# A feed forward phase whose slots close with the first layer's last product, and casts that follow their own gelu

## The chip, the cores and the metric

The kernel runs on one NeuronCore of one Trainium2 chip. The metric is the device time of one execution in microseconds. In this text PE is TensorE, DVE is VectorE, ACT is ScalarE, POOL is GpSimd and SP is SyncE, which here only issues DMA transfers.

## The reference

One transformer block over a batch of 32 sequences of 256 tokens, in fp32:

```
h = layernorm(x, ln1);  x = attention(h, h, sa_wq, sa_wk, sa_wv, sa_wo, sa_bo) + x
h = layernorm(x, ln2);  x = attention(h, ctx_768, ca_wq, ca_wk, ca_wv, ca_wo, ca_bo) + x
h = layernorm(x, ln3)
p = h @ ff_w1 + ff_b1                      # (256, 256) @ (256, 2048)
a, gate = p[..., :1024], p[..., 1024:]
x = (a * gelu(gate)) @ ff_w2 + ff_b2 + x   # (256, 1024) @ (1024, 256)
```

x is (32, 256, 256), the context (32, 256, 192), with 16 heads of 64. The change touches the last three lines only.

## The kernel before

A first phase, some 2300 us long, does both attentions for all batches and leaves x_ca in DRAM. A second phase does the feed forward, one batch (t) per iteration, 32 in all. Each engine's program is written by hand in its own order, and engines wait for each other by semaphores; nothing else sets the order of the work.

To keep fp32 accuracy, an operand is split into a high part, which PE can take in full (fp32r), and a remainder: hT_hi and hT_lo, w_hi and w_lo, a_hi and a_lo. One product of the mathematics is then three matmuls (high x high, high x low, low x high); `three` lists them. I call each matmul a product from here on. All of them here have a 128 x 128 stationary operand and 256 columns.

The 1024 hidden columns are cut into FT = 8 pieces. A slot of PE is one piece m: `hidden(t, m)` (12 products, into one of four banks of s_ps: 6 for the value half, 6 for the gate half), and `down`, which multiplies an earlier piece by its rows of ff_w2 (6 products: 3 into bank 0 of unit_ps for the first 128 tokens, 3 into bank 1 for the others, adding up over the 8 pieces). In slot m >= 2 it is down(t, m - 2), in slots 0 and 1 it is down(t - 1, 6) and down(t - 1, 7) of the batch before. The first iteration (START), which overlaps the end of attention, has an order of its own; the last (DRAIN) holds only the two last down pieces.

What hangs on a slot, with the semaphore that is raised:

- PE: the last product of hidden(m) raises p_full(m).
- ACT: `gelu(m)` waits for p_full(m), reads the gate half from s_ps and writes gate (gate_done). It is the line L895, ACT probs<-s_ps,b_col in the profile, since gate and hid lie in the buffer probs.
- DVE: `gated(m)` (L1080) adds the bias to the value half and multiplies by the gate into hid (hid_done).
- ACT: `hidden_hi(m)` (L900), the cast of hid to a_hi (u_hi). In the order of ACT it stands behind gelu(m + 1).
- POOL: `hidden_lo(m)` (L1268), a_lo = hid - a_hi (u_lo).
- PE: down(m), two slots on, waits for u_lo(m).

Other work of an iteration stands at fixed places of these orders. DVE: behind gated(0) it normalises the rows of batch t + 1 and transposes blocks of them (L1005, L1012); behind gated(1) it adds the residual to both banks of the finished batch t - 1 into x_out (L1202, y_done); behind gated(4) scale_rows (L1087, hT); behind gated(5) the statistics of batch t + 2 (L992); ahead of gated(6) the remainder hT_lo (L1094, rows_lo); behind gated(6) the moments mean_var (L997). ACT: behind the cast that follows gelu(5), the cast of hT to hT_hi (L904, `rows_hi`). POOL: behind a_lo(3) the residual addition x_rb (L1240, waits for the load of x_res); ahead of a_lo(6) `deviation` of batch t + 2 (var_eps, neg_mean, rstd, ln_shift, L1229 to L1234), in iterations 1 to 29. SP stores x_out when y_done allows, and loads x_res when that store has landed.

down(t, 0) starts a new sum in the banks of unit_ps, so it also waits for y_done: both additions of batch t - 1 must have read them. hidden(m) waits for hid_done(m - 4), the last reader of its bank.

## Time and profile before

| | us |
|---|---|
| median of 3 runs | 2865.33 (2865.15 to 2866.21) |
| the profiled execution | 2866.01 |
| its span, first to last instruction | 2864.2 |
| PE busy in the span | 2842.0, 25278 matmuls |
| DVE, ACT, POOL busy | 2256.3, 1912.3, 1471.1 |
| the feed forward stretch 2340 to 2844, PE busy | 504.00 of 504.00 |

The profile is of one execution. Start times are measured; the ends of matmuls are modelled, so the distance from one start to the next tells how fast products follow each other, and not the duration that stands with them (0.28 us). An engine's time without work is "idle"; a row shows in brackets how long the engine was idle ahead of it and who ended that.

### The profile page before, as it was taken

Reading aid. Unit: us, or ns where it says so; the run is one execution under the profiler, and the core shown is the slowest. Engines: PE = TensorE matmul, PEld = TensorE weight load, DVE = VectorE, ACT = ScalarE, POOL = GpSimd, SP = SyncE. Lnnn points to the kernel's source line nnn. Section 1 sums busy time; section 2 is a strip of 40 time slices with the busy share of each in tenths; the row PEclk is TensorE's granted clock in tenths of the full one; section 3 lists DMA queues with packets and bytes.
Section 4 is the critical chain, followed back from the end, with each engine's and each line's share of the span. In section 5 each row is a group of like instructions: output and inputs, shape, how many; then the busy total and the mean of one; then the engine's idle time right before and its main releaser. Section 6 shows DMA issues by size and latency. Waiting matters only on the chain.

```text
span 2864.2 us, 72446 instructions
## 1 busy us (share of the span) xinstructions
PE 2842.0 (99%) x25278; PEld 2485.3 (87%) x25278; DVE 2256.3 (79%) x3495; ACT 1912.3 (67%) x6041; POOL 1471.1 (51%) x1310
## 2 busy tenths in 40 slices
PE   8999999999999999999999999999999999999999
PEld 6888888888888888888888888888888889999999
DVE  6888888888888888888888888888888865555554
ACT  6677766677766776777777777777777754444443
POOL 5444444444444444765555555555555544554554
PEclk9999999999999999999999999999999999999999
DMA  5666666666666666667777776666766632222222
GB/s 147 158 162 157 156 157 159 158 154 145 151 151 154 150 148 149 161 166 177 177 172 169 173 171 169 168 164 165 168 168 163 151 100 88 73 73 84 81 73 63
DMA packets 355360, 413.32 MB, mean 144 GB/s; under 512 B 122048, under 2 KB 209472, under 8 KB 355264
## 3 DMA queue, kind: packets, MB, share of 16 engines
q1 hardware_dynamic: 345120, 395.29, 57.4%
q10 hardware_dynamic: 10144, 16.78, 1.6%
q8 instruction: 56, 0.92, 0.1%
q14 instruction: 40, 0.33, 0.0%
HBM read 94.52 MB, written 49.02 MB: 50 GB/s over the span
## 4 chain that ended last, share of the span: by engine, by line
PE 98%; DVE 1%; ACT 1%; POOL 0%; issue 0%; DMA 0%; DVEq 0%; POOLq 0%; ACTq 0%
PE unit_ps L593 54%; PE o_ps L618 17%; PE s_ps L606 14%; PE s_ps L593 12%; DVE neg_max L1021 0%; ACT probs L851 0%; DVE blocks L1035 0%; POOL probs L1253 0%; DMA x_ln<-in_x_dram 0%; ACT qk_hi L882 0%; DVE qk_lo L1046 0%; DVE hT L1016 0%; DVE hT_lo L1059 0%; ACT x_n L828 0%; ACT L828 0%
## 5 line engine op out<-in xcount | busy, mean ns | idle before, releaser
L1253 POOL TENSOR_TENSOR probs<-probs,row_inv 128x1024 f32<-128x1024 f32 x512 | 967.8, 1896 | 893.9 <-DVE row_inv L1026 893.9
L851 ACT ACTIVATE probs<-s_ps,neg_max 128x256 f32<-128x256 f32 x2048 | 950.4, 487 | 403.9 <-DVE neg_max L1021 403.4
L1021 DVE TENSOR_REDUCE neg_max<-s_ps 128x4 f32<-128x1024 f32 x512 | 616.8, 1205 | 62.8 <-PE s_ps L606 58.4
L1035 DVE STREAM_TRANSPOSE blocks<-probs 128x1024 f32<-128x1024 f32 x512 | 633.2, 1237 | 19.9 <-POOL probs L1253 19.9
L593 PE MATMUL unit_ps<-hT_hi,w_hi 128*128 128x256 f32 x2048 | 571.3, 282 | 3.0 <-DVE hT_lo L1059 2.6
L593 PE MATMUL unit_ps<-hT_hi,w_lo 128*128 128x256 f32 x2048 | 554.0, 277 | 0.0
L618 PE MATMUL o_ps<-pT,v_f 128*64 128x256 f32 x4096 | 498.5, 385 | 1.7 <-DVE a_lo L1041 1.7
L593 PE MATMUL unit_ps<-hT_lo,w_hi 128*128 128x256 f32 x1792 | 496.1, 277 | 0.0
L851 ACT ACTIVATION_READ_ACCUMULATOR probs<-s_ps,neg_max 128x1 f32 x2048 | 444.6, 217 | 0.0
L593 PE MATMUL unit_ps<-w_hi,a_hi 128*128 128x256 f32 x1536 | 430.8, 280 | 3.8 <-DVE a_lo L1041 2.8
L593 PE MATMUL unit_ps<-w_lo,a_hi 128*128 128x256 f32 x1536 | 425.7, 277 | 0.0
L593 PE MATMUL unit_ps<-w_hi,a_lo 128*128 128x256 f32 x1536 | 425.7, 277 | 0.0
L618 PEld LDWEIGHTS o_ps<-pT,v_f 128*64 128x64 f32 x4096 | 271.7, 136 | 174.6 <-issue 48.0
L1046 DVE TENSOR_TENSOR qk_lo<-unit_ps,qk_hi 128x512 fp32r<-128x512 f32 x512 | 350.8, 685 | 76.8 <-ACT qk_hi L882 62.5
L593 PEld LDWEIGHTS unit_ps<-hT_hi,w_hi 128*128 128x128 f32 x2048 | 384.3, 188 | 21.2 <-issue 1.5
L593 PEld LDWEIGHTS unit_ps<-hT_hi,w_lo 128*128 128x128 f32 x2048 | 384.6, 188 | 0.0
L593 PEld LDWEIGHTS unit_ps<-hT_lo,w_hi 128*128 128x128 f32 x1792 | 336.8, 188 | 5.7
L1268 POOL TENSOR_TENSOR a_lo<-probs,a_hi 128x256 fp32r<-128x256 f32 x256 | 188.3, 741 | 264.9 <-ACT a_hi L900 263.0
L895 ACT ACTIVATE probs<-s_ps,b_col 128x256 f32<-128x256 f32 x256 | 121.7, 476 | 300.2 <-PE s_ps L593 300.2
L606 PE MATMUL s_ps<-qk_hi 64*128 64x256 f32 x2048 | 315.2, 304 | 6.0 <-DVE qk_lo L1046 6.0
L882 ACT CAST qk_hi<-unit_ps 128x512 fp32r<-128x512 f32 x512 | 313.9, 613 | 6.4 <-PE unit_ps L593 4.6
L1080 DVE SCALAR_TENSOR_TENSOR probs<-s_ps,b_col,probs 128x256 f32<-128x256 f32 x256 | 123.4, 482 | 240.7 <-ACT probs L895 238.7
(73 smaller groups left out, 6017.8 us busy)
## 6 DMA issues: line engine op xcount, KB each, us to landing
pT<-blocks SPq DMA_DIRECT2D x1024, 256.0 KB, 4.5
rows_t_dram<-row_blocks SPq DMA_DIRECT2D x91, 256.0 KB, 4.4
rows_in<-rows_t_dram SPq DMA_DIRECT2D x91, 256.0 KB, 4.1
x_res<-in_x_dram SPq DMA_DIRECT2D x32, 256.0 KB, 4.1
x_sa_dram<-x_out SPq DMA_DIRECT2D x32, 256.0 KB, 4.3
x_ln<-x_sa_dram ACTq DMA_DIRECT2D x32, 256.0 KB, 4.9
ctx_in<-in_ctx_dram SPq DMA_DIRECT2D x32, 256.0 KB, 4.4
x_res<-x_sa_dram SPq DMA_DIRECT2D x32, 256.0 KB, 4.1
```

Of the source, the lines that this page charges most:

```text
L593: last = nc.tensor.matmul(dst, a, b, start=start and n == 0, stop=stop and n == len(terms) - 1)
L606: last = nc.tensor.matmul(s_ps[:, m % 2, hd, it * S:(it + 1) * S], q[part, r, 0, rows], k[part, r, 1, :], start=n == 0, stop=n == 2)
L618: last = nc.tensor.matmul(o_ps[part, i, :], v_f[:, jt, 2 * (2 * n + i) + hd, :], p[:, jt, hd], start=jt == 0, stop=jt == IT - 1)
L851: op = nc.scalar.activation(probs[:, m % 2, r, :].rearrange("p (j b c) -> p j b c", j=IT, c=BLK), scored.rearrange("p (j c b) -> p j b c", ...
L882: nc.scalar.copy(qk_hi[:, unit[1] % RING, :, :], bank.rearrange("p (a s) -> p a s", a=2)).then_inc(at.qk_hi, 1)
L895: nc.scalar.activation(gate[:, m % 2, :], s_ps[:, m % 4 // 2, m % 2, S:2 * S], ACT.Gelu, bias=b1_col[:, FT + m:FT + m + 1]).then_inc(ff.ga ...
L1021: nc.vector.tensor_reduce(neg_max[:, m % RING, :], s_ps[:, m % 2, :, :].rearrange("p h (i j) -> p (h i) j", j=S), AX_X, ALU.max, negate=Tr ...
L1035: nc.vector.transpose(blocks[:, n % 2, :, m % 2, :].rearrange("p b (j r c) -> p r j b c", j=IT, c=BLK), probs[:, m % 2, :, :].rearrange("p ...
L1046: nc.vector.tensor_tensor(qk_lo[:, m % RING, :, :], unit_ps[:, bank_of(("qk", m)), :].rearrange("p (a s) -> p a s", a=2), f32(qk_hi[:, m % ...
L1080: nc.vector.scalar_tensor_tensor(hid[:, m % 2, :], s_ps[:, m % 4 // 2, m % 2, 0:S], b1_col[:, m:m + 1], gate[:, m % 2, :], ALU.add, ALU.mu ...
L1253: nc.gpsimd.tensor_tensor(probs[:, m % 2, :, :], probs[:, m % 2, :, :], row_inv[:, m % RING, :].unsqueeze(2).broadcast_to([P, ROWS, S]), A ...
L1268: nc.gpsimd.tensor_tensor(a_lo[:, m, :], hid[:, m % 2, :], f32(a_hi[:, m, :]), ALU.subtract).then_inc(ff.u_lo, 1)
```

## The change

Three things change, all in the iterations of the feed forward behind the first:

- PE: hidden and down of a slot are no longer one behind the other. A slot is now 11 products of hidden, 5 of down, the last product of hidden (which raises p_full), the last product of down. The waits of down (u_lo, and for down(t, 0) also y_done) stand ahead of its first product, now the 12th of the slot. The number of products and their sums' order within each bank stay as they are.
- ACT: hidden_hi(m) now follows gelu(m), and not gelu(m + 1). At m = 5 the rows' cast rows_hi stands between the two.
- The first (START) and the DRAIN iteration keep their order, of PE and, in START, of ACT.

```
-            def hidden(t, m, parity):
...
+            def hidden_and_down(t, m, parity, b, d):
+
+                hidden_ready(t, m)
+                wide, narrow = hidden_terms(t, m, parity), down_terms(d)
+                run_terms(wide[:-1])
+                down_ready(b, d)
+                last = run_terms(narrow[:3])
+                if d == FT - 1:
+                    last.then_inc(ff.w2_full, 1)
+                run_terms(narrow[3:-1])
+                run_terms(wide[-1:]).then_inc(ff.p_full, 1)
+                last = run_terms(narrow[-1:])
+                if d == FT - 1:
+                    last.then_inc(ff.w2_full, 1)
...
                 for m in range(FT):
-                    if "cur" in parts and not (parts == START and m < BEGUN):
+                    if parts != START and "cur" in parts:
+                        hidden_and_down(t, m, parity, t if m >= 2 else t - 1, (m - 2) % FT)
+                        continue
+                    if "cur" in parts and m >= BEGUN:
                         hidden(t, m, parity)
...
                         gelu(t, m)
-                        if m:
+                        if parts == START:
                             hidden_hi(t, m - 1)
-                        if m == FT - 1:
-                            hidden_hi(t, m)
                     if "nxt" in parts and m == (FT - 2 if parts == START else FT - 3):
                         rows_hi(t + 1, 1 - parity)
+                    if "cur" in parts and (parts != START or m == FT - 1):
+                        hidden_hi(t, m)
```

`hidden_ready` and `down_ready` hold the waits that stood at the top of `hidden` and `down`, `hidden_terms` and `down_terms` list their 12 and 6 products in the order of before, and `run_terms` issues a list.

PE, in an iteration, from the last products of hidden(1) over down(t - 1, 7) to the start of slot 2; unit_ps<-w,a is down, s_ps<-hT,w is hidden. Before:

```order
L593 MATMUL s_ps<-hT_lo,w_hi 128x256
L593 MATMUL s_ps<-hT_hi,w_lo 128x256
L593 MATMUL unit_ps<-w_hi,a_hi 128x256 [waits ff_u_lo]
L593 MATMUL unit_ps<-w_lo,a_hi 128x256
L593 MATMUL unit_ps<-w_hi,a_lo 128x256
L593 MATMUL unit_ps<-w_hi,a_hi 128x256
L593 MATMUL unit_ps<-w_lo,a_hi 128x256
L593 MATMUL unit_ps<-w_hi,a_lo 128x256
L593 MATMUL s_ps<-hT_hi,w_hi 128x256 [waits ff_hid_done]
```

The same place in the changed kernel:

```order
L709 MATMUL s_ps<-hT_lo,w_hi 128x256
L709 MATMUL unit_ps<-w_hi,a_hi 128x256 [waits ff_u_lo]
L709 MATMUL unit_ps<-w_lo,a_hi 128x256
L709 MATMUL unit_ps<-w_hi,a_lo 128x256
L709 MATMUL unit_ps<-w_hi,a_hi 128x256
L709 MATMUL unit_ps<-w_lo,a_hi 128x256
L709 MATMUL s_ps<-hT_hi,w_lo 128x256
L709 MATMUL unit_ps<-w_hi,a_lo 128x256
L709 MATMUL s_ps<-hT_hi,w_hi 128x256 [waits ff_hid_done]
```

The product s_ps<-hT_hi,w_lo that raises p_full has moved down by five, and all of down but its last product has moved up by one. In slot 2 the first product of down also waits for ff_y_done, in both kernels.

ACT, from gelu(4) to gelu(6) of an iteration (ACTIVATE is gelu, CAST a_hi is hidden_hi, CAST hT_hi is rows_hi). Before:

```order
L895 ACTIVATE probs<-s_ps,b1_col 128x256 [waits ff_hid_done,ff_p_full]
L900 CAST a_hi<-probs 128x256 [waits ff_hid_done]
L895 ACTIVATE probs<-s_ps,b1_col 128x256 [waits ff_hid_done,ff_p_full]
L900 CAST a_hi<-probs 128x256 [waits ff_hid_done]
L904 CAST hT_hi<-hT 128x512 [waits ff_h_done]
L895 ACTIVATE probs<-s_ps,b1_col 128x256 [waits ff_hid_done,ff_p_full]
```

The same stretch in the changed kernel:

```order
L936 ACTIVATE probs<-s_ps,b1_col 128x256 [waits ff_hid_done,ff_p_full]
L941 CAST a_hi<-probs 128x256 [waits ff_hid_done]
L936 ACTIVATE probs<-s_ps,b1_col 128x256 [waits ff_hid_done,ff_p_full]
L945 CAST hT_hi<-hT 128x512 [waits ff_h_done]
L941 CAST a_hi<-probs 128x256 [waits ff_hid_done]
L936 ACTIVATE probs<-s_ps,b1_col 128x256 [waits ff_hid_done,ff_p_full]
```

The cast behind each gelu is now that of the same m, where it was that of m - 1; the one that belongs to gelu(5) stands behind the rows' cast.

## Rows read from the trace of the kernel before

**Rows 1.** The page: PE's busy time, its clock in 40 slices, the chain by engine.
```profile
PE 2842.0 (99%) x25278; PEld 2485.3 (87%) x25278; DVE 2256.3 (79%) x3495; ACT 1912.3 (67%) x6041; POOL 1471.1 (51%) x1310
...
PEclk9999999999999999999999999999999999999999
...
PE 98%; DVE 1%; ACT 1%; POOL 0%; issue 0%; DMA 0%; DVEq 0%; POOLq 0%; ACTq 0%
```

**Rows 2.** Busy us (x instructions) by engine, clock, DMA share, GB/s, 2340 to 2844.
```profile
2340.00:2844.00 504.00, 504.00 (x4343) 504.00 (x4342) 277.60 (x597) 207.49 (x512) 252.72 (x392) 1.00 0.26 78
```

**Rows 3.** PE's timeline, slots 1 and 2: start us, duration, engine, line, operation.
```profile
2526.01 0.28 PE L593 MATMUL s_ps<-hT_hi,w_hi 128*128 128x256 f32 x1
...
2527.31 0.28 PE L593 MATMUL s_ps<-hT_hi,w_lo 128*128 128x256 f32 x1
...
2528.14 0.28 PE L593 MATMUL s_ps<-hT_hi,w_hi 128*128 128x256 f32 x1
...
2529.39 0.28 PE L593 MATMUL s_ps<-hT_hi,w_lo 128*128 128x256 f32 x1
```

**Rows 4.** DVE's timeline: gated(1), x_out twice; scale_rows behind gated(4); mean_var behind gated(6).
```profile
2528.14 0.48 DVE L1080 SCALAR_TENSOR_TENSOR probs<-s_ps,b_col,probs 128x256 f32<-128x256 f32 x1
2528.54 0.74 DVE L1202 TENSOR_TENSOR x_out<-unit_ps,x_rb 128x256 f32<-128x256 f32 x2
...
2534.80 2.13 DVE L1087 TENSOR_SCALAR hT<-rows_in,ln_gain,ln_bias 128x256 f32<-128x256 f32 x2
...
2539.02 0.24 DVE L997 BATCH_NORM_AGGREGATE mean_var<-bn 128x2 f32<-128x6 f32 x2
```

**Rows 5.** PE's timeline: the start of slot 3, and down(6) in the next slot 0.
```profile
2530.19 0.28 PE L593 MATMUL s_ps<-hT_hi,w_hi 128*128 128x256 f32 x1
...
2542.05 0.28 PE L593 MATMUL unit_ps<-w_hi,a_hi 128*128 128x256 f32 x1
```

**Rows 6.** POOL's timeline: a_lo(0), the residual, the deviation's start, a_lo(6), the program's last.
```profile
2528.47 0.74 POOL L1268 TENSOR_TENSOR a_lo<-probs,a_hi 128x256 fp32r<-128x256 f32 x1 [2.74 <-ACT a_hi L900]
...
2535.43 1.35 POOL L1240 TENSOR_TENSOR x_rb<-x_res,out_bias 128x512 f32<-128x512 f32 x1
...
2539.61 0.20 POOL L1229 TENSOR_TENSOR var_eps<-mean_var,eps 128x2 f32<-128x2 f32 x1
...
2541.01 1.44 POOL L1268 TENSOR_TENSOR a_lo<-probs,a_hi 128x256 fp32r<-128x256 f32 x2
...
2858.67 1.42 POOL L1268 TENSOR_TENSOR a_lo<-probs,a_hi 128x256 fp32r<-128x256 f32 x2 [1.34 <-ACT a_hi L900]
```

**Rows 7.** ACT's timeline: gelu(1), the cast behind it, the rows' cast, the last cast.
```profile
2527.63 0.48 ACT L895 ACTIVATE probs<-s_ps,b_col 128x256 f32<-128x256 f32 x1 [1.54 <-PE s_ps L593]
2528.00 0.40 ACT L900 CAST a_hi<-probs 128x256 fp32r<-128x256 f32 x1
...
2536.96 0.62 ACT L904 CAST hT_hi<-hT 128x512 fp32r<-128x512 f32 x1 [0.21 <-DVE hT L1087]
...
2858.85 0.40 ACT L900 CAST a_hi<-probs 128x256 fp32r<-128x256 f32 x1 [0.26 <-DVE probs L1080]
```

**Rows 8.** PE's timeline at the program's end: down products behind a wait.
```profile
2859.45 0.39 PE L593 MATMUL unit_ps<-w_hi,a_hi 128*128 128x256 f32 x1 [0.98 <-POOL a_lo L1268]
2859.68 0.28 PE L593 MATMUL unit_ps<-w_lo,a_hi 128*128 128x256 f32 x1
2859.80 0.28 PE L593 MATMUL unit_ps<-w_hi,a_lo 128*128 128x256 f32 x1
```

**Rows 9.** SP's timeline: the load of x_res is issued.
```profile
2531.68 0.38 SPq L578 DMA_DIRECT2D x_res<-x_ca_dram  x1
```

**Rows 10.** PE's timeline where the phases meet: the products behind a long wait.
```profile
2313.05 0.55 PE L593 MATMUL unit_ps<-w_hi,a_hi 128*128 128x256 f32 x1 [2.81 <-DVE a_lo L1041]
2313.40 0.41 PE L593 MATMUL unit_ps<-w_lo,a_hi 128*128 128x256 f32 x1
...
2315.32 0.41 PE L593 MATMUL unit_ps<-w_lo,a_hi 128*128 128x256 f32 x1
```

More of the change, by code:

```diff
@@ L702, in down, with hidden @@
                     at_least(pe, ff.y_done, IT * b)
-                for it, bank in enumerate((unit_ps[:, 0, :], unit_ps[:, 1, :])):
-                    rows = slice(it * P, (it + 1) * P)
-                    last = product(bank[:, 0:D], three(a_hi[:, m, rows], a_lo[:, m, rows],
-                                                       w_hi[:, 2, m * D:(m + 1) * D], w_lo[:, 2, m * D:(m + 1) * D]),
-                                   start=m == 0, stop=m == FT - 1)
+            def hidden(t, m, parity):
+                hidden_ready(t, m)
+                run_terms(hidden_terms(t, m, parity)).then_inc(ff.p_full, 1)
+            def down(b, m):
+                down_ready(b, m)
+                terms = down_terms(m)
+                for part in (terms[:3], terms[3:]):
+                    last = run_terms(part)
                     if m == FT - 1:
                         last.then_inc(ff.w2_full, 1)
+            def hidden_and_down(t, m, parity, b, d):
+                hidden_ready(t, m)
+                wide, narrow = hidden_terms(t, m, parity), down_terms(d)
[9 more added lines that the diff above has]
+                    last.then_inc(ff.w2_full, 1)
             def transpose_rows(b):
@@ L776, in iteration @@
                         pe.wait_ge(ff_w2_lo, 1)
-                    if "cur" in parts:
-                        for d in {4: (0,), 5: (1,), 6: (2, 3), 7: (4, 5)}.get(m, ()) if parts == START else (m - 2,) if m >= 2 else ():
+                    if parts == START:
+                        for d in {4: (0,), 5: (1,), 6: (2, 3), 7: (4, 5)}.get(m, ()):
                             down(t, d)
@@ L967, in iteration @@
                         gelu(t, m)
-                        if m:
+                        if parts == START:
                             hidden_hi(t, m - 1)
-                        if m == FT - 1:
-                            hidden_hi(t, m)
                     if "nxt" in parts and m == (FT - 2 if parts == START else FT - 3):
                         rows_hi(t + 1, 1 - parity)
+                    if "cur" in parts and (parts != START or m == FT - 1):
+                        hidden_hi(t, m)
             over_batches(act, B, iteration)
```

32 lines of the change are left out of this document (23 added, 9 removed).

## The prediction

> **What bounds the kernel now.** I read the page's engine table and its chain of waits first: TensorE (PE) is busy 99% of the span and is 98% of the chain that ended last [rows 1]. Then the busy time of the feed forward stretch, which is all that the change touches: from 2340 to 2844 us PE is busy in all 504.00 us, with 4343 products at a granted clock of 1.00, while VectorE (DVE) has 278, ScalarE (ACT) 207 and GpSimd (POOL) 253 us [rows 2]. So nothing waits on PE's side, and a product costs 504.0 / 4343 = 0.116 us. An iteration is 8 slots x 18 products = 144 products, or 16.7 us. That leaves two ways for the order of products to cost or gain: it changes how fast products follow each other, or it makes PE wait for data that today arrive just in time. I call the product that raises p_full(m) "p(m)": before, it is the 12th of slot m, after, the 17th.
>
> The reader is to see in PE's own rows how little is spare. In the slot m = 2 shown, the last product ahead of down(0) starts at 2529.39, and with it the load of down(0)'s weights [rows 3]. down(0) overwrites the two banks that DVE's x_out additions read, so it waits for y_done, and the second addition ends at 2528.54 + 0.74 = 2529.28 [rows 4]. The spare time is 0.11 us. Slot m = 0 is alike: down(6) begins at 2542.05 [rows 5], its load a product earlier, at 2541.93, and the remainder a_lo of product 6, the first of a pair that takes 1.44 us in sum from 2541.01 [rows 6], ends near 2541.75: 0.18 us spare.
>
> **Part 1: p_full comes 5 products later.** No product is added or taken away. p(m) moves from place 12 to place 17, so it comes 5 x 0.116 = 0.58 us later in its slot, and gelu(m), gated(m) and everything behind them on DVE shift with it. At the same time down's first product moves from place 13 to place 12, so its data are needed 0.12 us earlier. Together: everything that hangs on p(m) and is needed by a down product loses 0.70 us. What hung on p(m-1) and is now cut loose from it is part 2.
>
> The addition that frees the banks is hit in full. Its chain: p(1) starts at 2527.31 [rows 3], gelu(1) at 2527.63 [rows 7], gated(1) at 2528.14, the two additions to 2529.28 [rows 4]; that is 1.97 us from p(1). DVE's order puts the additions of iteration t behind gated(t, 1) and the change leaves this so; the casts on ACT play no part. Before, p(1) to the load of down(0) is 18 products, 2529.39 - 2527.31 = 2.08 us. After, it is from place 17 of slot 1 to the start of the 11th product of slot 2, 12 products, 12 x 0.116 = 1.39 us. PE is late by 1.97 - 1.39 = 0.58 us. A product that waited starts 0.04 us after its release: the a_lo pair that ends at 2858.67 + 0.74 = 2859.41 for its first [rows 6] lets PE go at 2859.45, and the next product follows 0.23 us on [rows 8]; in the stream it is also two products, 0.23 us, from the start of a load to that next product, so nothing more is lost. Stall: 0.58 + 0.05 (with rounding) = 0.63 us. It stands in every iteration that has both a current and a previous batch, 31 of 32: **31 x 0.63 = 19.5 us**. Behind the waiting product are queued 4 more of down(0) and p(2); so gelu(2) comes later too, but slots 2 to 7 keep their distances, and nothing is caught up, since PE has no idle time in which to do so.
>
> **Part 2: each cast follows its own gelu.** Before, cast(m-1) is run after gelu(m). Left so, a_lo(m) would end 2.0 us after p(m+1) (from p(1) at 2527.31 to 2528.47 + 0.74 = 2529.21 is 1.90 [rows 3, 6]) against 1.39 us given, and all slots would stall by 0.5 us. With cast(m) behind gelu(m), the chain for a clean m is, from p(m): 0.32 to gelu, 0.51 to gated, 0.48 for gated, 0.03 and 0.40 for the cast (as after the last gated, [rows 7]), 0.07 to POOL (2528.00 + 0.40 to 2528.47), 0.74 for a_lo: 2.55 us [rows 3, 4, 6, 7]. It is given from place 17 of slot m to place 11 of slot m+2, 30 products, 3.48 us. So 0.9 us is spare, and the cast costs nothing in a clean slot: ACT is idle there for 1.54 us of a slot [rows 7]. Three slots are not clean:
>
> m = 4: the residual addition on POOL stands ahead of a_lo(4). Its input x_res is asked for at 2531.68 [rows 9], 4.37 us after p(1), and has landed by 2535.43 [rows 6], 8.12 us after p(1). Now p(1) to p(4) is 3 slots and the stall, 6.9 us, so the addition starts at the latest 1.2 us after p(4), takes 1.35, and a_lo(4) ends at 3.3 us after p(4), where 3.48 are given. No cost.
>
> m = 5: ACT now runs the rows' cast, which waits for scale_rows (hT), ahead of cast(5). p(4) is 73 products ahead of the product at 2542.05 [rows 5], at 2533.58; hT ends at 2534.80 + 2.13 = 2536.93 [rows 4], 3.35 us after it; the rows' cast adds 0.65, cast(5) 0.40, a_lo(5) 0.81 [rows 6, 7]: 5.2 us from p(4), 3.1 from p(5), against 3.48. No cost, 0.4 us spare.
>
> m = 6: POOL's deviation of batch t+2 (var_eps to ln_shift) stands ahead of a_lo(6), and it waits for DVE's mean_var, which stands behind gated(6). p(6) lies 37 products ahead of the one at 2542.05 [rows 5], at 2537.75. From there mean_var ends at 2539.02 + 0.24 = 2539.26, or 1.51 [rows 4]; POOL picks it up 0.07 later, at 1.58 (before, it was busy with a_lo(5) until 2539.61; that cover is gone since a_lo(5) now comes earlier); from var_eps to a_lo is 2541.01 - 2539.61 = 1.40, giving 2.98; a_lo(6) takes 0.74: 3.72; with 0.05 for the release 3.77 us [rows 6]. Given are 3.48. Stall: 0.29 us, in the iterations t = 1 to 29, which are those with a deviation: **29 x 0.29 = 8.4 us**. Its bounds: 0.2 if POOL picks up at once and rows_lo no longer holds gated(6) back by 0.05 us, 0.4 if each semaphore takes 0.05 more.
>
> **Part 3: the end.** The last batch's gelu(7) comes 0.58 us later; its a_lo(7), queued until 2860.09 behind a_lo(6) today [rows 6], ends at 2858.85 + 0.58 (the cast's new start [rows 7]) + 0.48 + 0.74 = 2860.65: **0.6 us** at the end.
>
> **Part 4: the pace.** Slots alternate: the one from 2526.01 takes 2.13 us and the next, from 2528.14, 2.05 us (products 0.118 and 0.113 apart) [rows 3, 5]. The turn comes at a slot's first product, where PE goes from unit_ps to s_ps, whichever pace it leaves; at the opposite crossing none is seen. The new order has two crossings of each kind per slot. I can't derive what it does: if each crossing to s_ps turns the pace, 16 of 18 products keep the pace of the slot before, and all may be fast or all slow. After a wait, a down product restarts at 0.118 [rows 8], which speaks for slow. Of 144 products, 42 (12 and 30) lie in the two stretches whose length the chains set, so the pace counts in 102: all fast gives 31 x 8 x 0.037 x 102 / 144 = -6.5 us, all slow +6.5 us, alternating 0. I take 0, since both ends have the same reach, and keep both for the range.
>
> **The sum.** 19.5 + 8.4 + 0.6 + 0 = 28.5 us on the profiled execution's own time of 2866.01 us (span 2864.2 and 1.8 around it), 2894.5 us. The median of the runs, 2865.33, lies 0.7 below that execution: **2893.8 us**, or 1.0% slower.
>
> **The rivals.**
> (a) Both stalls, all slots slow: 2893.8 + 6.5 = 2900 us. For it: the restart pace, and two turns in a slot, which would keep a pace once taken. Against: that slots alternate today.
> (b) Both stalls, all slots fast: 2887 us.
> (c) Only the y_done stall, because mean_var reaches POOL sooner: 2893.8 - 8.4 = 2885 us. Against it: the 1.40 us from var_eps to a_lo are POOL's own.
> (d) At the start of the phase 9 products take 2315.32 - 2313.40 = 1.92 us, 0.2133 us each [rows 10], at half speed. The pace falls to half of that, 0.1067 us: the new order would take out what makes them 0.113 or 0.118 at full speed. 102 x 31 x 0.0094 = 29.7 us are given back, and the kernel ends at 2864 us, **not slower**; the deciding pace is 0.116 - 28.5 / 3162 = 0.107 us. Against it: no row of the stretch shows such a pace for 256 columns with a load for each. The Trainium skill ("TensorE: Matmul & The Clock Gate", on the back-to-back issue gap) gives N / 2.4 GHz + 2.5 ns and says that loading the next weights steals nothing from the running matmul, which would be 0.109 us whatever the order; the trace shows 0.113 and 0.118 here, so the rule does not hold for this stream. With that figure the estimate would be 2872 us.
> (e) More stalls than I found, or the clock: after an idle time of 2.81 us PE's products come 0.213 us apart, at half their pace [rows 10]. A stall of 0.63 us is far from that, and the page shows 9 tenths or more in each slice of the clock's row [rows 1], but if each stall brought some of it, 2905 to 2960 us.
> (f) The change doing nothing: excluded, the order of PE and ACT differs in each slot.
>
> **How the numbers follow.** Forecast with mixed pace 0.55 (2889 to 2899); (a) 0.13; (b) 0.12; (c) 0.08; (d) 0.05, half of it near 2872, half near 2864; (e) 0.06; 0.01 for some faster way. The range leaves out (d), (e) and a little of (a): 2884 to 2904. A measurement of this kernel tells 0.2% (5.7 us, 2859.6 to 2871.1) from no change; slower 0.94, same 0.04, faster 0.02.
>
> **What would show it.** In the changed profile, PE should have idle time put down to DVE x_out in slot 2 (31 times, near 0.6 us) and to POOL a_lo in slot 0 (29 times, near 0.3); PE busy in the same stretch should fall to about 95%; iterations should last 17.6 us, not 16.7; var_eps should start about 0.07 after mean_var. The gelu should start in the slot's last product. Wrong would be: no PE wait on x_out, which breaks the largest term; waits in other slots, which means that a chain was missed; slots that all last 2.05 or 2.13 us, which decides part 4.

## The result, and the profile after

| | before | after |
|---|---|---|
| median, us | 2865.33 (2864.28 to 2866.85, 5 executions) | 2895.32 (2893.77 to 2895.58, 5 executions) |
| the profiled execution | 2866.01 | 2895.32 |
| its span | 2864.2 | 2893.5 |

The changed kernel takes 1.0103 times as long, interval 1.0089 to 1.0117. The forecast was 2893.8 us in a range of 2884 to 2904.

The page of the changed kernel: PE's line of the engine table, its clock in 40 slices, the chain by engine and by line. They answer [rows 1].

```profile
PE 2862.0 (99%) x25278; PEld 2493.0 (86%) x25278; DVE 2251.0 (78%) x3495; ACT 1931.2 (67%) x6041; POOL 1468.7 (51%) x1310
...
PEclk9999999999999999999999999999999999999999
...
PE 96%; DVE 2%; ACT 1%; issue 1%; POOL 0%; DMA 0%; DVEq 0%; POOLq 0%; ACTq 0%
PE unit_ps L593 48%; PE o_ps L618 16%; PE s_ps L606 14%; PE s_ps L709 11%; PE unit_ps L709 7%; DVE x_out L1243 1%; ACT probs L936 1%; DVE neg_max L1062 0%; ACT probs L892 0%; DVE blocks L1076 0%; POOL probs L1294 0%; DMA x_ln<-in_x_dram 0%;
```

The clock's row has not changed, the number of products neither. What is new is in the chain: PE had 98% of it and has 96%, and DVE's x_out, which was not in it, has 1%.

PE's waits in the feed forward phase of the changed kernel: in total, times, the longest.

```profile
PE unit_ps L709 <- DVE x_out L1243: 10.7, 31, 0.5
PE unit_ps L709 <- POOL a_lo L1309: 1.1, 1, 1.1
```

The 31 waits for x_out are there. The 29 waits for a_lo in slot 0 are not (the one listed is that of the program's end), and the 31 are listed at 0.35 us each in the mean and not at 0.6. Both come from the same thing: the end of a product is modelled at 0.28 us behind its start, while in the stream the next one starts after 0.116. A wait shows as idle time only by what it exceeds this 0.16 us. The list of the weight loads (PEld), from 2340 to 2880, has both:

```profile
PEld unit_ps L709 <- DVE x_out L1243: 15.1, 28, 0.6
PEld unit_ps L709 <- POOL a_lo L1309: 6.0, 29, 0.2
PEld unit_ps L709 <- issue: 1.8, 3, 0.6
```

28 and 3 (which the profile puts down to no releaser) are the 31 of slot 2, and the 29 of slot 0 are there. A load shows as taking 0.19 us, so these times are too short as well; for the size of a stall the starts have to be read. PE's timeline of the changed kernel around slot 2 of one iteration: start us, duration, engine, line, operation, idle before. It answers [rows 3].

```profile
2520.82 0.28 PE L709 MATMUL s_ps<-hT_hi,w_lo 128*128 128x256 f32 x1
...
2521.05 0.28 PE L709 MATMUL s_ps<-hT_hi,w_hi 128*128 128x256 f32 x1
...
2522.23 0.28 PE L709 MATMUL s_ps<-hT_lo,w_hi 128*128 128x256 f32 x1
2522.85 0.39 PE L709 MATMUL unit_ps<-w_hi,a_hi 128*128 128x256 f32 x1 [0.33 <-DVE x_out L1243]
2523.07 0.28 PE L709 MATMUL unit_ps<-w_lo,a_hi 128*128 128x256 f32 x1
...
2531.92 0.28 PE L709 MATMUL s_ps<-hT_hi,w_lo 128*128 128x256 f32 x1
...
2535.41 0.28 PE L709 MATMUL s_ps<-hT_lo,w_hi 128*128 128x256 f32 x1
2535.69 0.39 PE L709 MATMUL unit_ps<-w_hi,a_hi 128*128 128x256 f32 x1
2535.92 0.28 PE L709 MATMUL unit_ps<-w_lo,a_hi 128*128 128x256 f32 x1
```

2520.82 is p(1). From the last product ahead of down(0) to down(0) is 2522.85 - 2522.23 = 0.62 us and to the next product 0.22 more, 0.84 in all where the stream takes 0.23: the stall is 0.61 us. p(6) is at 2531.92, and down(6) at 2535.69 comes 0.28 us after its predecessor and 0.23 ahead of its successor, 0.51 in place of 0.23: a stall of 0.28 us with no bracket behind it.

From here on a stall is this: the time from the last product ahead of down's first to the second of down, less 0.23 us.

The chain of the first stall, DVE and then ACT, same kernel and view; it answers [rows 4, 7].

```profile
2521.65 0.48 DVE L1121 SCALAR_TENSOR_TENSOR probs<-s_ps,b_col,probs 128x256 f32<-128x256 f32 x1
2522.05 0.74 DVE L1243 TENSOR_TENSOR x_out<-unit_ps,x_rb 128x256 f32<-128x256 f32 x2
...
2521.14 0.47 ACT L936 ACTIVATE probs<-s_ps,b_col 128x256 f32<-128x256 f32 x1 [0.47 <-PE s_ps L709]
2522.16 0.41 ACT L941 CAST a_hi<-probs 128x256 fp32r<-128x256 f32 x1 [0.55 <-DVE probs L1121]
```

gelu(1) starts 0.32 us after p(1), gated(1) 0.51 later, the additions end at 2522.05 + 0.74 = 2522.79, 1.97 us after p(1), to the hundredth what it was before. PE starts 0.06 us later. The cast at 2522.16 isn't in this chain.

The chain of the second: POOL, then DVE, same kernel. It answers [rows 4, 6]; a_lo(5) is the row at 2531.63, a_lo(6) the one at 2534.89.

```profile
2528.13 1.29 POOL L1281 TENSOR_TENSOR x_rb<-x_res,out_bias 128x512 f32<-128x512 f32 x1
...
2531.63 0.73 POOL L1309 TENSOR_TENSOR a_lo<-probs,a_hi 128x256 fp32r<-128x256 f32 x1 [1.34 <-ACT a_hi L941]
2533.54 0.20 POOL L1270 TENSOR_TENSOR var_eps<-mean_var,eps 128x2 f32<-128x2 f32 x1 [1.18 <-DVE mean_var L1038]
...
2534.89 0.75 POOL L1309 TENSOR_TENSOR a_lo<-probs,a_hi 128x256 fp32r<-128x256 f32 x1
...
2528.96 1.49 DVE L1128 TENSOR_SCALAR hT<-rows_in,ln_gain,ln_bias 128x256 f32<-128x256 f32 x2
...
2531.81 1.11 DVE L1135 TENSOR_TENSOR hT_lo<-hT,hT_hi 128x512 fp32r<-128x512 f32 x1
2532.84 0.47 DVE L1121 SCALAR_TENSOR_TENSOR probs<-s_ps,b_col,probs 128x256 f32<-128x256 f32 x1
2533.24 0.23 DVE L1038 BATCH_NORM_AGGREGATE mean_var<-bn 128x2 f32<-128x6 f32 x2
```

POOL had been idle for 1.18 us when mean_var released it, 0.07 us after its end; a_lo(6) ends at 2535.64, 3.72 us after p(6).

At the end, on POOL and then PE, same kernel: the last remainder and the product that waits for it ([rows 6, 8] before).

```profile
2888.72 0.72 POOL L1309 TENSOR_TENSOR a_lo<-probs,a_hi 128x256 fp32r<-128x256 f32 x1 [1.38 <-ACT a_hi L941]
...
2889.49 0.38 PE L709 MATMUL unit_ps<-w_hi,a_hi 128*128 128x256 f32 x1 [1.13 <-POOL a_lo L1309]
```

The whole difference of the two profiled executions, 29.3 us, can be laid out from the starts:

| where | us |
|---|---|
| slot 2, 31 stalls, 27 of them 0.61 and four 0.63 to 0.69 | 19.1 |
| slot 0, 29 stalls of 0.27 to 0.30 | 8.1 |
| the pace of the products: from the second slot of the phase to the last slot 7 are 554.75 us and not 526.40, less the stalls | 1.1 |
| from the start of the last slot 7 to the last product, 5.17 and not 4.60 | 0.6 |
| ahead of the changed code (the second slot of the phase starts at 2330.25 and not 2329.85) | 0.4 |
| sum | 29.3 |

### The profile page after: what moved, and what is told of

Its sections match the earlier page's. It is cut to its first block, busy times and chain, and to the rows that moved or that the text cites. A ratio compares the mean times of both kernels' runs of the same rounds, so it can differ in the third digit from the quotient of the medians.

```text
span 2893.5 us, 72446 instructions
## 1 busy us (share of the span) xinstructions
PE 2862.0 (99%) x25278; PEld 2493.0 (86%) x25278; DVE 2251.0 (78%) x3495; ACT 1931.2 (67%) x6041; POOL 1468.7 (51%) x1310
## 4 chain that ended last, share of the span: by engine, by line
PE 96%; DVE 2%; ACT 1%; issue 1%; POOL 0%; DMA 0%; DVEq 0%; POOLq 0%; ACTq 0%
PE unit_ps L593 48%; PE o_ps L618 16%; PE s_ps L606 14%; PE s_ps L709 11%; PE unit_ps L709 7%; DVE x_out L1243 1%; ACT probs L936 1%; DVE neg_max L1062 0%; ACT probs L892 0%; DVE blocks L1076 0%; POOL probs L1294 0%; DMA x_ln<-in_x_dram 0%; ACT qk_hi L923 0%; PE unit_ps L796 0%; DVE probs L1121 0%
## 5 line engine op out<-in xcount | busy, mean ns | idle before, releaser
L902 ACT CAST a_hi<-o_ps 128x512 fp32r<-128x512 f32 x256 | 153.6, 600 | 210.9 <-PE o_ps L618 210.1
L593 PE MATMUL unit_ps<-w_hi,a_hi 128*128 128x256 f32 x1024 | 287.8, 281 | 2.8 <-DVE a_lo L1082 2.8
L606 PE MATMUL s_ps<-qk_lo,qk_hi 64*128 64x256 f32 x2048 | 289.0, 279 | 0.0
L606 PE MATMUL s_ps<-qk_hi,qk_lo 64*128 64x256 f32 x2048 | 288.2, 278 | 0.0
```

Source lines behind the costliest of these rows:

```text
L593: last = nc.tensor.matmul(dst, a, b, start=start and n == 0, stop=stop and n == len(terms) - 1)
L606: last = nc.tensor.matmul(s_ps[:, m % 2, hd, it * S:(it + 1) * S], q[part, r, 0, rows], k[part, r, 1, :], start=n == 0, stop=n == 2)
L902: nc.scalar.copy(a_hi[:, 2 * n:2 * n + 2, :], o_ps[:]).then_inc(at.a_hi_done, 1)
```

## The experiments

All times in us, the kernel before beside each on the same chip (its medians lay between 2865.15 and 2865.76). The ratio is to it, with its interval; it is an estimate from all executions and need not be the quotient of the two medians.

| kernel | median (lowest to highest, executions) | ratio |
|---|---|---|
| e3_casts_alone | 2866.75 (2865.50 to 2867.16, 10) | 1.0004 (0.9994 to 1.0013) |
| e4_products_alone | 2988.12 (2987.68 to 2988.56, 2) | 1.0425 (1.0404 to 1.0446) |
| e1_additions_first | 2885.57 (2883.64 to 2888.27, 4) | 1.0068 (1.0051 to 1.0085) |
| e2_remainder_first | 2870.17 (2868.13 to 2871.37, 10) | 1.0015 (1.0006 to 1.0025) |
| e8_rows_remainder_later | 2886.53 (2883.67 to 2886.83, 4) | 1.0070 (1.0053 to 1.0087) |
| e5_two_of_down | 2880.95 (2875.98 to 2882.08, 4) | 1.0056 (1.0039 to 1.0073) |
| e5b_two_of_down_again | 2877.49 (2876.17 to 2879.65, 3) | 1.0043 (1.0027 to 1.0059) |
| e6_before_one_wait_less | 2866.37 (2863.91 to 2866.55, 10) | 1.0002 (0.9992 to 1.0012) |
| e7_both_mended_one_wait_less | 2869.68 (2869.11 to 2872.72, 10) | 1.0018 (1.0009 to 1.0028) |
| e9_mended_three_of_down | 2867.50 (2866.93 to 2868.59, 10) | 1.0006 (0.9997 to 1.0016) |
| e10_mended_four_of_down | 2875.38 (2872.93 to 2878.83, 6) | 1.0035 (1.0022 to 1.0048) |
| e11_mended_two_of_down | 2864.41 (2862.67 to 2874.24, 12) | 1.0009 (0.9999 to 1.0018) |

### The two halves of the change apart

The casts alone, on the kernel before:

```
-                        if m:
+                        if parts == START:
                             hidden_hi(t, m - 1)
-                        if m == FT - 1:
-                            hidden_hi(t, m)
...
+                    if "cur" in parts and (parts != START or m == FT - 1):
+                        hidden_hi(t, m)
```

> The kernel before, with only ACT's part of the change: each cast follows its own gelu, PE's order is that of before. Theory: casts cost nothing and gain nothing, since PE did not wait for a_lo: 2865.3 us (2864 to 2867), within 0.1% of before. The end is the same too, since the last a_lo hangs on gelu(7). Rival (ACT waiting for gated delays gelu or the rows' cast, and so PE): 2 to 10 us slower.

Measured: 2866.75 us, within the range given, and no difference that can be told. One thing did move: hT_lo on DVE takes 1.24 us (median of 30) where it took 0.69, since a_lo(5) now runs beside it on POOL. That it costs nothing shows how much room the old order of products leaves on that side.

The products alone, the changed kernel with ACT's old order:

```
-                        if parts == START:
+                        if m:
                             hidden_hi(t, m - 1)
+                        if m == FT - 1:
+                            hidden_hi(t, m)
...
-                    if "cur" in parts and (parts != START or m == FT - 1):
-                        hidden_hi(t, m)
```

> The changed kernel with ACT's order of before: cast(m-1) behind gelu(m), only the products are moved. Theory: a_lo(m-1) ends 1.90 us after p(m), with 0.05 for the release 1.95, and 12 products = 1.39 us are given, so every slot of 31 iterations stalls by 0.56 us, slot 2 by 0.63, slot 0 a little more for the deviation: 31 x (7 x 0.56 + 0.63) + 2 = 143 us over before, about 3008 us (2995 to 3025). Rival (the cast's place is of no weight, the cost is in the products' order and y_done): within 5 us of 2895.

PE's waits in this kernel over the whole span:

```profile
PE unit_ps L709 <- POOL a_lo L1309: 54.6, 186, 1.5
PE unit_ps L709 <- DVE x_out L1243: 10.9, 31, 0.4
```

Measured: 2988.12 us, 20 less than expected. The size of a stall was right, 0.55 us from start to start. Their number was not: 186 is 6 x 31, and with slot 2 that makes 7 of 8 slots. Slot 1, which takes down(t - 1, 7), runs through, because in the old order too the cast of the last piece stands right behind its own gelu(7). 31 x (6 x 0.555 + 0.61) = 122 us; measured are 123.0 over the kernel before. So the order of casts is worth nothing by itself and 93 us under the new order of products (2988.1 to 2895.3): the change needs both halves, and the loss is that of the products.

### The slot-2 stall, and what stood behind it

The two additions ahead of gated(t, 1) on DVE, in the changed kernel:

```
+                    if m == 1 and "prv" in parts:
+                        dve.wait_ge(ff.xrb_done, t)
+                        for it, bank in enumerate((unit_ps[:, 0, :], unit_ps[:, 1, :])):
+                            dve.wait_ge(ff.w2_full, IT * (t - 1) + it + 1)
+                            nc.vector.tensor_tensor(x_out[:, it, :], bank[:, 0:D], x_rb[:, it, :], ALU.add).then_inc(ff.y_done, 1)
                     if "cur" in parts and not (parts == START and m < BEGUN):
                         gated(t, m)
...
-                    if m == 1 and "prv" in parts:
...
```

> The changed kernel, but on DVE the two x_out additions of batch t-1 stand ahead of gated(t, 1), not behind it. Theory (two chains hung on p_full make PE wait): the y_done wait of slot 2 goes. The second addition now waits only for the last product of slot 1 and ends about 0.28 + 0.04 + 0.42 = 0.74 us after its start, where 11 products = 1.28 us are given. The changed kernel's profile has 31 gaps of 0.61 us over a normal step there, 18.8 us: 2895.3 - 18.8 = 2876.5 us (2875 to 2878). Rival (the mixed order of products is itself slow, and the waits only fall where PE is late anyway): the time stays within 3 us of 2895.

PE's waits in e1 from 2330 to 2890:

```profile
PE unit_ps L709 <- POOL a_lo L1309: 10.0, 24, 1.1
```

The timeline of e1 in one iteration, POOL's rows and then DVE's. x_rb is the residual addition of the iteration's own batch, hT is scale_rows:

```profile
2507.41 1.29 POOL L1281 TENSOR_TENSOR x_rb<-x_res,out_bias 128x512 f32<-128x512 f32 x1 [0.69 <-DMA x_res<-x_ca_dram]
...
2510.63 0.73 POOL L1309 TENSOR_TENSOR a_lo<-probs,a_hi 128x256 fp32r<-128x256 f32 x1 [1.19 <-ACT a_hi L941]
2512.54 0.20 POOL L1270 TENSOR_TENSOR var_eps<-mean_var,eps 128x2 f32<-128x2 f32 x1 [1.18 <-DVE mean_var L1038]
...
2507.50 2.10 DVE L1128 TENSOR_SCALAR hT<-rows_in,ln_gain,ln_bias 128x256 f32<-128x256 f32 x2
...
2510.68 1.23 DVE L1135 TENSOR_TENSOR hT_lo<-hT,hT_hi 128x512 fp32r<-128x512 f32 x1
2511.84 0.47 DVE L1121 SCALAR_TENSOR_TENSOR probs<-s_ps,b_col,probs 128x256 f32<-128x256 f32 x1
```

Measured: 2885.57 us, 9 more than expected. The wait for x_out is gone, as expected, and 10 us are gone with it, not 19. The stall in slot 0 has grown: by the starts it is between 0.17 and 0.88 us, 16.5 us over 29 iterations or 0.57 in the mean, where it was 0.28; in this iteration down(6) comes 0.72 us after its predecessor (2513.95 to 2514.67). The rows show why. p(6) is at 2510.47 here. gated(6) starts 1.37 us after it, and 0.92 us after it in the changed kernel. Of these 0.45 us, 0.32 are a later start of hT_lo (0.21 after p(6), not 0.11 ahead of it) and 0.12 its longer run (1.23, not 1.11). The later start goes back to scale_rows: here POOL's residual addition waits for the load of x_res, and seen from p(4), two slots ahead of p(6), it starts 0.7 us later than in the changed kernel, where the stall of slot 2 had given the load time. It now lies beside the whole of scale_rows (2507.41 beside 2507.50, hT in 2.10 us), where in the changed kernel it began 0.83 us ahead of it (2528.13 and 2528.96, hT in 1.49 us). In slot 2 0.05 to 0.08 us are left over in 28 iterations (2.1 us in all), since the additions there stand behind the transposes of slot 0.

The 0.32 and 0.12 are read off one iteration; the cause shows in all 29 of this trace. In 22 of them x_rb starts 0.86 to 1.30 us after p(4), and the later it starts the longer is the stall of slot 0, nearly one for one: 0.47 us at 0.86, 0.61 at 1.01, 0.78 at 1.19, 0.88 at 1.30. In one it starts 0.40 us after p(4), as in the changed kernel, and the stall is 0.28. In the other six the load lands so late that x_rb starts 1.31 us or more after p(4) and scale_rows has begun ahead of it, at 1.23 us; hT then takes 1.73 us or less and the stall is 0.26 us or less. One of these six, POOL's row and then DVE's:

```profile
2490.59 1.28 POOL L1281 TENSOR_TENSOR x_rb<-x_res,out_bias 128x512 f32<-128x512 f32 x1 [1.02 <-DMA x_res<-x_ca_dram]
2490.30 1.73 DVE L1128 TENSOR_SCALAR hT<-rows_in,ln_gain,ln_bias 128x256 f32<-128x256 f32 x2
```

So the stall of slot 0 in e1 is set by when the load of x_res lands, which the stall of slot 2 had hidden. Whether hT_lo is the part that decides was tried next but one.

e2: the same, and on POOL the remainder ahead of the deviation:

```
+                    if "cur" in parts:
+                        hidden_lo(t, m)
                     if m == FT - 2 and rows_ahead(t, parts) and parts != START:
                         deviation(ff, t + 2)
-                    if "cur" in parts:
-                        hidden_lo(t, m)
```

> As the first, and on POOL a_lo(6) stands ahead of the deviation of batch t+2, not behind it. Theory: the slot 0 stall, 29 gaps of 0.28 us, 8.1 us, goes too: 2868.4 us (2866.5 to 2870), which leaves about 0.6 us for the end and 1 to 2 us for the extra crossings between the two sets of banks. No PE wait is left in the stretch. Rival (the order of products costs by itself): 2876 or more.

Measured: 2870.17 us. This is just above the range given. With both stalls out of the way, the new order of products costs 5.0 us. In the profiled execution 4.8 us lie between the two kernels: 2.0 are the 0.07 us left in slot 2 28 times, 0.7 five waits in slot 6, 1.3 the pace, 0.5 the end, and 0.3 lie ahead of the changed code. So the two chains named in the prediction are nearly all there was: from the changed kernel to this one are 25 us, and the two terms had 27.9.

The waits in slot 6 are a third chain, that of the prediction's m = 4: the load of x_res, x_rb, a_lo(4), down(4). The longest of them, on POOL and then on the weight loads:

```profile
2352.28 1.45 POOL L1281 TENSOR_TENSOR x_rb<-x_res,out_bias 128x512 f32<-128x512 f32 x1 [1.21 <-DMA x_res<-x_ca_dram]
2354.49 0.19 PEld L709 LDWEIGHTS unit_ps<-w_hi,a_hi 128*128 128x128 f32 x1 [0.30 <-POOL a_lo L1309]
```

Here x_rb starts 1.65 us after p(4), and the stall is 0.37 us; the four others are 0.09 us. In the changed kernel, where the stall of slot 2 comes first, x_rb starts at most 0.59 us after p(4) and slot 6 never waits.

e8: e1, and DVE's hT_lo behind gated(6) and the moments:

```
-                    if (m == FT - 2 and by_blocks(t, parts)) or (m == FT - 1 and parts == START):
+                    if m == FT - 1 and parts == START:
                         rows_lo(t + 1, 1 - parity)
...
                     if m == FT - 2 and rows_ahead(t, parts):
                         norm_moments(ff)
+                    if m == FT - 2 and by_blocks(t, parts):
+                        rows_lo(t + 1, 1 - parity)
```

> The kernel with the x_out additions ahead of gated(1) (e1_additions_first, 2885.6 us, 9 us above what its theory gave, with a new PE wait of 0.5 to 0.7 us on a_lo(6) in slot 0), and on DVE rows_lo of batch t+1 now behind gated(6) and the moments, not ahead of them. Theory C (rows_lo, drawn out to 1.20 us where POOL's a_lo(5) runs beside it, against 0.69 us alone, holds gated(6) back, and through the deviation a_lo(6)): gated(6) starts 0.83 us after p_full(6)'s product and not 1.37, the wait in slot 0 shrinks from about 0.6 to about 0.25 us, and 29 x 0.3 to 0.5 us are given back: 2874 us (2871 to 2878). Rival (the wait comes from POOL's own order, which the deviation fills): 2884 to 2887.

The timeline of e8 where mean_var meets the deviation, DVE's rows and then POOL's:

```profile
2513.06 0.24 DVE L1038 BATCH_NORM_AGGREGATE mean_var<-bn 128x2 f32<-128x6 f32 x2
2513.22 0.66 DVE L1135 TENSOR_TENSOR hT_lo<-hT,hT_hi 128x512 fp32r<-128x512 f32 x1
...
2513.38 0.55 POOL L1272 TENSOR_TENSOR var_eps<-mean_var,eps 128x2 f32<-128x2 f32 x1 [0.53 <-DVE mean_var L1038]
```

The deviation's first operation over all iterations of e8 (min, median, max in ns):

```profile
L1272 POOL TENSOR_TENSOR var_eps<-mean_var,eps x29: 548/550/552, 2356.8 to 2843.8; 128x2 f32<-128x2 f32 x29
```

Measured: 2886.53 us, the rival's number. hT_lo no longer holds gated(6), and takes 0.66 us and not 1.24. But the operation of two columns that follows on POOL, 0.20 us in every other kernel here, takes 0.55, for it starts inside hT_lo and ends 0.05 us behind its end (2513.88 and 2513.93). The stall in slot 0 is 0.55 us, 16.0 us over all, where e1 had 16.5; it is now nearly alike in all iterations (0.52 to 0.60 us), whenever the load lands. The cost was moved from one engine to the other. So hT_lo on DVE and var_eps on POOL can't run side by side, and in the two places tried for hT_lo something ahead of a_lo(6) is late; what removed the stall was to take the deviation from ahead of a_lo(6) (e2).

### p_full a little earlier

e5: the last product of hidden after 2 products of down and not 5. The edit, in hidden_and_down of the changed kernel:

```
-                last = run_terms(narrow[:3])
+                run_terms(narrow[:2])
+                run_terms(wide[-1:]).then_inc(ff.p_full, 1)
+                last = run_terms(narrow[2:3])
...
-                run_terms(narrow[3:-1])
-                run_terms(wide[-1:]).then_inc(ff.p_full, 1)
-                last = run_terms(narrow[-1:])
+                last = run_terms(narrow[3:])
```

> The changed kernel with the last product of hidden moved three places up: 11 of hidden, 2 of down, the last of hidden (place 14), the last 4 of down. Theory (lateness grows product by product): from p_full(1) to down(0)'s load are now 15 products = 1.74 us against the chain of 2.02, a stall of 0.27 us in slot 2, 31 x 0.27 = 8.4 us; in slot 0 33 products = 3.83 us against 3.77, no stall. 2865.3 + 8.4 + 0.4 for the end + 1 for the crossings = 2875 us (2873 to 2878). If DVE's rows_lo is again drawn out by POOL's a_lo beside it, slot 0 adds up to 29 x 0.3 us, 2884. Rival (the order of products costs by itself, wherever p_full stands): 2890 or more.

> e5_two_of_down once more, for a second profile: its runs lay between 2876 and 2882 us, and its profile, of a 2876 run, showed 141 slots of 2.08 us and 56 of 2.12. Theory: the pace that a slot settles in differs between executions, the difference of 5 us being some 130 more slots of 2.12 us. If this profile is of a run near 2881, it has 100 or more slots of 2.12 us, or else more waiting; if it is near 2876 it looks as the first.

Measured: 2880.95 and, once more, 2877.49 us. Three products (0.35 us) given back per slot take the slot-2 stall from 0.61 to 0.28 us in the mean (0.25 to 0.35, 8.6 us in all), and the time falls by 14 to 18 us. In slot 0 the stall is gone in about half of the iterations; 16 have one of 0.04 to 0.58 us, 2.9 us in all (13 and 2.2 us in the second profile), and as in e1 it is there when x_rb starts late. The direction and the stall are as the chains say. The time lies between what the two readings gave, and its spread over seven executions, 6 us, is wider than any other's up to here. The second profile, of the 2877.49 us execution, has 84 slots of 2.12 and 2.13 us where the first, of 2875.98 us, has 60, some 1.0 us of the 1.5 between them; no execution above 2880 us was profiled, so the spread was not settled here. The next kernels bear on it.

### The pace

Two ideas of what turns the pace at a slot's first product were set against each other with e6: the wait for hid_done that stands there, or the order of products itself. e6 is the kernel before and e7 is e2, each with that wait in the first iteration only (the order of the bank is kept without it: down of the slot before has waited for an a_lo that comes after that hid_done). The edit of e6; in e7 the same line reads `t * FT + m - 3`:

```
-                at_least(pe, ff.hid_done, g - 3)
+                if t == 0 if isinstance(t, int) else False:
+                    at_least(pe, ff.hid_done, g - 3)
```

> The kernel before, without PE's wait for hid_done at each slot's first product, behind the first iteration (it is implied: down of the slot before has waited for the a_lo that follows that hid_done). No other edit. Theory A (the wait on the first load of a slot is what turns the pace between 0.113 and 0.118 us): all slots keep one pace, 2865.3 - 9.2 = 2856 us if all are fast, 2874.5 if all are slow. Theory B (going from unit_ps to s_ps, that is from down to hidden, turns it): the slots alternate as before, 2865 us within 1.5 us.

> The kernel with both stalls mended (x_out additions ahead of gated(1), a_lo(6) ahead of the deviation, measured 2870.2 us), and without the hid_done wait. Theory A: one pace throughout, about 2861 or 2879 us. Theory B: 2870 us within 1.5 us.

Measured: 2866.37 and 2869.68 us, each the same as the kernel it was made from, and the slots of e6 still last 2.05 and 2.13 us in turn (122 of each). The wait doesn't turn the pace.

e9, e10 and e11 are e2 with the last product of hidden after 3, 4 and 2 products of down:

```
-                run_terms(narrow[3:-1])
                 run_terms(wide[-1:]).then_inc(ff.p_full, 1)
-                last = run_terms(narrow[-1:])
+                last = run_terms(narrow[3:])
```

(e9; in e10 `narrow[3:4]` stays ahead of it, e11 has e5's edit.)

> Both mends (additions ahead of gated(1), a_lo(6) ahead of the deviation), and the slot is 11 of hidden, 3 of down, the last of hidden, 3 of down. Theory D (a crossing from down to hidden turns the pace if enough products follow; three turn it back before the next slot's first product): no waits, slots of 2.076 us each instead of 2.053 and 2.127 in turn, 248 x (2.090 - 2.076) = 3.5 us less and 0.35 us more at the end: 2862 us, or 2872 if slots settle in the slow pace (2.116 us). Rival (the turn is tied to the slot and not to the crossing): slots alternate, 2867 us.

> As e9_mended_three_of_down with 4 of down ahead of the last of hidden and 2 behind it. Theory D with two products enough for a turn: slots of 2.072 us, 2861 us. If two are too few: slots of 2.067 and 2.126 us in turn, as in the changed kernel, 2867 us.

> Both mends (additions ahead of gated(1), a_lo(6) ahead of the deviation), and the slot is 11 of hidden, 2 of down, the last of hidden, 4 of down. No waits are expected. What the pace does was not foretold right for 3 and 4 of down (slots of 2.07 and 2.12 us in turn; all of 2.13). With 2 of down the profiles of e5 show slots that keep 2.08 us until a wait throws them into 2.12. Theory D: without waits all keep 2.08: 2865.5 - 248 x 0.010 + 0.25 = 2863 us. If they settle at 2.12: 2873 us. Rival (without the waits they alternate like the others): 2867 us.

Busy us (x instructions) by engine from 2500 to 2840, of e2, e9, e10 and e11, in this order, one fence each; PE's count is the number of products that fit into 340 us.

```profile
2500.00:2840.00 340.00, 340.00 (x2910) 339.87 (x2910) 192.14 (x401) 152.68 (x344) 168.97 (x263) 1.00 0.26 79
```

```profile
2500.00:2840.00 340.00, 340.00 (x2922) 340.00 (x2921) 193.50 (x406) 153.90 (x346) 170.31 (x263) 1.00 0.26 78
```

```profile
2500.00:2840.00 340.00, 340.00 (x2872) 340.00 (x2871) 191.06 (x400) 150.96 (x339) 166.50 (x259) 1.00 0.26 76
```

```profile
2500.00:2840.00 340.00, 340.00 (x2945) 340.00 (x2944) 193.97 (x406) 154.76 (x348) 172.01 (x265) 1.00 0.26 78
```

The same stretch of the kernel before, and of the changed one:

```profile
2500.00:2840.00 340.00, 340.00 (x2931) 340.00 (x2929) 189.45 (x406) 140.78 (x347) 170.64 (x264) 1.00 0.26 78
```

```profile
2500.00:2840.00 340.00, 333.61 (x2776) 325.51 (x2774) 176.27 (x388) 145.76 (x328) 160.43 (x250) 1.00 0.25 73
```

With no wait in this stretch, e9, e10 and e11 still differ. The lengths of slots, from start to start, with how many there are from 2340 us to the last slot (246 or 247):

| kernel | slots |
|---|---|
| before | 2.05 (123), 2.08 (1), 2.13 (123) |
| changed | 2.06 to 2.08 (121), 2.12 and 2.13 (66); with a stall 2.39 and 2.40 (29), 2.72 to 2.77 (31) |
| e9 (3 of down ahead) | 2.07 (124), 2.12 (123) |
| e10 (4) | 2.12 and 2.13 (243), 2.06 and 2.09 (1 each); with a wait in slot 6 2.42 (1) |
| e11 (2) | 2.08 (246); with a wait in slot 6 2.25 (1) |

The pace also turns within a slot. In e11, in the mean of its slots, the first three distances are 0.117 to 0.123 us, the next ones 0.113, and from the crossing to the last product of hidden it is back at 0.117 to 0.120; so does the shorter slot of e9. In the changed kernel that same crossing costs one product 0.120 us and does not turn the pace; in e10 there is hardly a fast slot to see it in.

e9 alternates as before and lands at 2867.50, the rival's number. e10 has nearly only long slots, 2875.38, which neither expectation gave. e11 was profiled in an execution of 2864.36 us with 246 slots of 2.08, as its theory had it; but its twelve executions fall into two groups, seven from 2862.67 to 2864.45 and five from 2870.78 to 2874.24, and no execution of the second group was profiled. The distance, 9.8 us between the middles of the groups, is that between all slots at 2.08 and all near 2.12 (246 x 0.04 = 10), which is an argument and not a measurement; waits in the second group are not excluded. So the pace of the stream hangs on the order of products, it can hold for all slots or change with each, and one and the same order (e11) has given two times, which may be two paces. What in the order decides it stays open. No kernel of this study is measurably faster than the one before: e11's ratio is 1.0009 (0.9999 to 1.0018).

## Why the prediction was right, step by step

**The y_done chain, 19.5 us.** Measured 19.1. Every link came as read from before: p(1) to the end of the additions 1.97 us, twelve products given, the restart 0.06 us after. The 0.02 us per stall are within the rounding.

**The a_lo(6) chain, 8.4 us.** Measured 8.1. a_lo(6) ends 3.72 us after p(6), as worked out, and var_eps starts 0.07 us after mean_var's end. The sum is as exact as that by two small errors that cancel: mean_var ends 1.55 us after p(6) and not 1.51, and from var_eps to a_lo(6) are 1.35 us and not 1.40. And that the first is so small was partly luck: the prediction put rows_lo at 0.05 us at most, with hT_lo as long as before. The change made hT_lo 1.11 us long and not 0.69, because the earlier cast brings a_lo(5) beside it. This was offset by an earlier start of hT_lo, 0.11 us ahead of p(6) and not 0.26 behind it, since scale_rows was shorter (hT in 1.49 us and not 2.13): x_rb, which lies beside it before, now starts 0.40 us after p(4) and not 1.86, as a_lo(3) is done earlier and the stall of slot 2 gives the load of x_res its time. e1 took that time away and the stall became 0.57 us in the mean. The prediction sees chains; that two operations beside each other on DVE and POOL change each other's length was not in it, and it is the main mechanism that was missed.

**The end, 0.6 us.** Measured 0.56, from the start of the last slot 7 to the last product.

**The pace, 0.** Measured +1.1 us. Slots go on alternating, also across stalls, and so rivals (a) and (b) fell: the second crossing to s_ps, ahead of the product that raises p_full, does not turn the pace in this order. That was not derived, the prediction took 0 as the middle of what it could not tell. What was left out is that the fast slots are not as fast: 2.07 us and not 2.05, since their crossings between hidden and down cost up to 0.12 us each where the stream has 0.113. Of the bounds, the upper one is borne out in size: e10, where nearly all slots last 2.13 us, is 9.6 us above the kernel before, over all 144 products of an iteration and not 102. The lower one is not reached by any kernel here: all of e11's slots at 2.08 us are 2.5 us less than before's 2.05 and 2.13 in turn, where all at 2.05 would have been about 9.

**No stall in the other slots.** Right for this kernel: its loads show 31 waits in slot 2, 29 in slot 0 and no other. For m = 5 there was more room than the 0.4 us given, about 0.9: a_lo(5) ends at 2532.36, 2.56 us after p(5), and 3.48 are given. For m = 4 the reading rests on the stall of slot 2, as the prediction's 6.9 us say; in e2, which has no such stall, slot 6 waits in five iterations.

**Rival (d)**, that the new order would bring products 0.107 us apart: no stretch shows it, the fastest stream found is e11's 340 / 2945 = 0.1154. The 0.109 us that the prediction took from the Trainium skill ("TensorE: Matmul & The Clock Gate", "Back-to-back issue gap") were the wrong figure to weigh: the section gives that formula for a matmul by itself and says that in a stream of loads and matmuls both set the distance, and of the next weights' load the page says that it takes no SBUF read bandwidth from the running matmul, not that it is without effect. The 0.1154 to 0.1184 us measured here do not contradict it. **Rival (e)**: the clock of the stretch stays at 1.00, and after a wait of 0.61 us the next products come 0.22, 0.12, 0.12 us apart; the stalls cost their own length.

**What the prediction said would be seen, and wasn't.** PE's busy share of the stretch was to fall to 95%; it is 517.67 of 528.00 us, 98%:

```profile
2340.00:2868.00 528.00, 517.67 (x4312) 505.66 (x4311) 272.15 (x595) 225.90 (x508) 250.45 (x390) 1.00 0.25 74
```

The count tells what the share hides: 528.00 / 4312 = 0.1224 us for a product, where [rows 2] have 0.1160, 5% less. And the waits of slot 0 are not in PE's list of waits, only in that of its loads. Iterations last 17.65 us, as said.

**The aside of part 2**, that without the moved casts all slots would stall by 0.5 us, was wrong by one slot (e4), since cast(7) is its own case in the old code; the stall is 0.55 us, as its own 1.90 us give, and not 0.5, which comes from the 2.0 beside them.

## What to carry to other kernels

In an engine that never waits, count for every semaphore that it raises the products from there to the first one that needs what hangs on it, and compare with the chain read from the timeline; moving the signal later costs nothing until the spare time is used up, and then the whole rest in each iteration. After one such wait is removed, work out the next chain anew with its neighbours in mind: of the 19 us of slot 2, removing its wait gave back only 10, because the wait had also given a load the time to land, and so kept work of two engines apart. Find the waits of a saturated TensorE in the list of its weight loads, and their size in the distance of starts and the count of products in a stretch, not in its busy share.

## What the runs showed of the hardware

- DVE and POOL can hold each other up. hT_lo, which reads two SBUF tiles, takes 0.69 us with POOL idle (before, from 2538.01), 1.11 us when it starts 0.18 us behind a_lo(5) (2531.81 and 2531.63), and 1.23 when 0.05 behind (2510.68 and 2510.63). In both it ends 0.55 to 0.56 us after the end of a_lo(5) (2532.92 and 2532.36; 2511.91 and 2511.36), as if it had done little until then. The other way round, var_eps takes 0.55 in place of 0.20 when it starts inside hT_lo. The Trainium skill ("SBUF — State Buffer", on who interferes with whom) says that a VectorE instruction with two SBUF inputs and a GpSimd instruction that reads SBUF contend, that the first to start holds the shared ports for its whole length and that the second fully blocks. The three cases agree. hT_lo over the iterations of the changed kernel (min, median, max in ns):

```profile
L1135 DVE TENSOR_TENSOR hT_lo<-hT,hT_hi x29: 1106/1108/1110, 2355.4 to 2849.5; 128x512 fp32r<-128x512 f32 x29
```

- The products of one and the same shape, in a stream without waits, came 0.1154 (e11), 0.1160 (before), 0.1164 (e9) or 0.1184 us (e10) apart on average in the profiled executions, at a granted clock of 1.00; the order of the products is what differs. For e11 five of twelve executions were some 10 us longer, and none of them was profiled.
- A wait of 0.61 us costs TensorE nothing beyond itself: no change of the granted clock, and the distance of the second product after it is the stream's.
